# Unrolled rounds of 512 samples, eight looked-up tables, and gathers paced by TensorE's progress in a DLRM tower on one core

## What is computed

```python
e = jnp.stack([tbl_0[ids[:, 0]], ..., tbl_25[ids[:, 25]]], axis=1)
combined = jnp.concatenate([dense[:, None, :], e], axis=1)          # 2048 x 27 x 128
inter = jnp.einsum('bfd,bgd->bfg', combined, combined)[:, triu_i, triu_j]
h = jnp.concatenate([dense, inter, dense], axis=1)                  # 128 + 351 + 128
h = jnp.maximum(h @ W_top1 + b_top1, 0.0)                           # 512
h = jnp.maximum(h @ W_top2 + b_top2, 0.0)                           # 256
y = h @ W_top3                                                      # 1
```

## Time and profile before

| | |
|---|---|
| timed runs, us | 488.62, 491.50, 497.02 (median 491.5) |
| span of the profiled execution, us | 791.1 (granted TensorE clock 0.756 of full) |
| PE busy | 487.2 us, 62% |
| PEld busy | 424.6 us, 54% |
| DVE busy | 226.9 us, 29% |
| ACT busy | 262.0 us, 33% |
| POOL busy | 305.1 us, 39% |

### The profile page before, as it was taken

How to read it: one execution, slowest core, us unless ns; L and a number is a source line. 1 busy time by engine, 2 the same in 40 slices (tenths; PEclk the granted TensorE clock), 3 DMA queues, 4 the chain that set the end, 5 groups by cost and what they waited for, 6 DMA issues and landing times.

```text
span 791.1 us, 8476 instructions
## 1 busy us (share of the span) xinstructions
PE 487.2 (62%) x3016; PEld 424.6 (54%) x3016; DVE 226.9 (29%) x296; ACT 262.0 (33%) x632; POOL 305.1 (39%) x327
## 2 busy tenths in 40 slices
PE   6407566526748086580956719476393855939977
PEld 4306556426637085470855518464282745827866
DVE  3207251222313142321413213133131332313231
ACT  1115131512416033160522615025150432405762
POOL 6751707370442606336072541705327071350000
PEclk8757767666959679596886959768596866958997
DMA  5620202110110101111010110101101020010000
GB/s 128 198 72 11 54 7 55 28 52 9 34 37 19 53 1 45 27 24 46 0 50 20 35 35 9 52 10 40 30 17 50 3 53 17 27 43 1 1 1 0
DMA packets 20003, 27.57 MB, mean 35 GB/s; under 512 B 10940, under 2 KB 13508, under 8 KB 19985
## 3 DMA queue, kind: packets, MB, share of 16 engines
q0 software_dynamic: 10240, 20.99, 10.3%
q1 hardware_dynamic: 9728, 6.32, 2.9%
q10 hardware_dynamic: 16, 0.01, 0.0%
HBM read 27.29 MB, written 0.01 MB: 35 GB/s over the span
## 4 chain that ended last, share of the span: by engine, by line
PE 42%; another core or an unknown queue 22%; issue 20%; ACT 12%; DVE 3%; DMA 0%; ACTq 0%; SPq 0%; DVEq 0%
PE gram L415 16%; PE ring L453 12%; PE ring L372 11%; ACT xt L585 6%; ACT pairs_or_h L606 4%; DVE onehot L705 2%; PE idb L361 1%; PE ring L442 1%; PE ring L476 1%; ACT xt L574 1%; ACT A L592 1%; DMA pairs_t_or_h<-in_ids 0%; DVE A L786 0%; DVE x_or_h_split L772 0%
## 5 line engine op out<-in xcount | busy, mean ns | idle before, releaser
L321 POOL DMA_INDIRECT rows<-in_tbl,ids_tile x320 | 304.3, 951 | 401.6 <-PE ring L400 306.7
L415 PE MATMUL gram<-xt 128*128 128x104 f32 x1024 | 161.4, 318 | 31.6 <-issue 28.3
L415 PEld LDWEIGHTS gram<-xt 128*128 128x128 f32 x1024 | 153.1, 233 | 38.5 <-issue 33.6
L372 PE MATMUL ring<-onehot,table_hi 125*128 125x256 f32 x368 | 113.1, 334 | 37.6 <-DVE onehot L705 31.3
L705 DVE TENSOR_TENSOR onehot<-idb,vrow 125x2048 fp32r<-125x2048 f32 x48 | 110.0, 2292 | 59.8 <-remote 47.2
L453 PE MATMUL ring<-x_or_h_split,w_hi 128*128 128x256 f32 (+1 forms) x384 | 95.6, 322 | 47.9 <-issue 40.2
L785 DVE COPY A<-gram 32x208 f32<-32x208 f32 x64 | 32.2, 503 | 309.6 <-remote 171.3
L591 ACT COPY A<-gram 32x208 f32<-32x208 f32 x64 | 32.4, 506 | 244.4 <-remote 163.9
L453 PEld LDWEIGHTS ring<-x_or_h_split,w_hi 128*128 128x128 f32 (+1 forms) x384 | 74.1, 219 | 64.0 <-issue 56.8
L372 PEld LDWEIGHTS ring<-onehot,table_hi 125*128 125x128 f32 x368 | 79.9, 217 | 48.0 <-issue 40.2
L372 PE MATMUL ring<-onehot,table_lo 125*128 125x256 f32 x368 | 103.7, 308 | 1.4 <-issue 1.4
(11 more groups left out here) (46 smaller groups left out, 272.9 us busy)
## 6 DMA issues: line engine op xcount, KB each, us to landing
rows<-in_tbl,ids_tile POOLq DMA_INDIRECT x320
xt<-in_tbl SPq DMA_DIRECT2D x6, 500.0 KB
rows<-in_r_dense_features SPq DMA_DIRECT2D x16, 64.0 KB
A<-in_W_top SPq DMA_DIRECT2D x2, 256.0 KB
xt<-in_W_top SPq DMA_DIRECT2D x2, 256.0 KB
pairs_or_h<-in_W_top SPq DMA_DIRECT2D x1, 512.0 KB
ids_tile<-in_ids SPq DMA_DIRECT2D x16, 13.0 KB
pairs_t_or_h<-in_ids SPq DMA_DIRECT2D x1, 208.0 KB
```

Of the source, the lines that this page charges most:

```text
L321: pool.indirect_dma_start(rows[:, t % 2, 1 + r, :], None, aps[f"tbl_{f}"], bass.IndirectOffsetOnAxis(ap=ids_tile[:, t, f:f + 1].bitcast(U3 ...
L372: last = pe.matmul(ps[:, 0:HALF], part[:, m, k, :], onehot[:, buf, k, :], start=(k == 0 and part is table_hi), stop=(k == KT - 1 and part ...
L415: last = pe.matmul(gram[:, s % 2, g // PER_BANK, col:col + QUAD * NA], four, cols, start=True, stop=True)
```

## The change

The stage list is one straight list without hardware loops, over four rounds of 512 samples, with pieces of several stages laid between each other. Two more tables (15 and 19) are looked up, so 18 are gathered: 288 gathers. A lookup serves 512 samples: 16 matmuls of 512 columns, 32 lookups in all instead of 48. The ids reach PSUM otherwise: SP loads them from a transposed copy of `ids`, broadcast to 128 partitions, and ACT copies them to PSUM, to `idb` and a bank of `gram` in turn. The one-hots are made in four quarters (125x1024) in three slots. The gathered rows live in a ring of 45 rows, with a semaphore for every six gathers of a tile, and each six gathers also wait until PE has filled as many ring banks as `PACE` says. Layers 1 and 2 are plain float32 without a split (`w1`, `w2`, `x`, `h1` whole); `W_top1` has its pair rows permuted on the host, since the looked-up tables now stand last among the features, so ACT stores each bank of transposed rows in one copy. DVE copies three of four product blocks and some strips of the pairs, ACT the rest. Each ring bank has a semaphore of its own. The raw tables are loaded in two pieces, 112 and 13 partitions. The cleared pads of XT are one instruction on DVE.

```diff
-LOOKUP_TABLES = [2, 5, 10, 12, 13, 14]
+LOOKUP_TABLES = [2, 5, 10, 12, 13, 14, 15, 19]
+ROWS = 45
+GROUP = 6
+PACE = [(0, -2.0), (48, 58.0), (138, 166.0), (282, 354.0)]
...
+        def a_round(r):
+            q, last = r - 1, r == NB - 1
+            for m in range(NL):
+                yield "lookup", r, m, 0
+                if q > 0 and m in (0, 1):
+                    yield from layer("layer2", q, 0, m)
+                if q > 0 and m == 2:
+                    yield from layer("layer3", q, 0, 0)
+                if m in (2, 3):
+                    yield from layer("unblock", q, 1, 2 * m - 4, 2 * m - 3)
+                if m == 4:
+                    yield from layer("pairs", q, 1, 0, 1, 2)
+                if m in (5, 6):
+                    yield from layer("layer1", q, 1, m - 5)
+                    yield from rows(r, 0, m - 5)
...
+            for s in range(TSTEPS):
+                yield "products", r, 2, s
+                yield from rows(r, 3, s)
+                yield from layer("unblock", r, 0, s)
...
+    EARLY_CHUNKS = [(2, 1), (3, 1), (3, 3)]
+    def on_vector(r, h, b):
+        return b % 2 == 1 and (h == 0 or r == NB - 1)
...
+                for part in (slice(0, VP16), slice(VP16, VP)):
+                    sp.dma_start(raw[m][part], src[part]).then_inc(raw_landed[m], 16)
...
+            for m in range(3, NL + 1):
+                spread_ids(m)
             W1, W2 = aps["W_top1"], aps["W_top2"]
+            sp.wait_ge(lo_ready, NL)
+            sp.dma_start(w1[:, 0], W1[0:D, :]).then_inc(w1_landed, 16)
...
+            sp.wait_ge(w1_ready, 1)
+            sp.dma_start(w2[:], W2.rearrange("(k p) n -> p k n", p=P)).then_inc(weights_landed, 16)
...
+                    i = k * NG + g
+                    if i >= ROWS and (g == 0 or group_of(i - ROWS) != group_of(i - ROWS - 1)):
+                        pool.wait_ge(ring_filled, filled("rows", *group_of(i - ROWS)))
+                    if i % GROUP == 0 and progress_for(i, k) > 0:
+                        pool.wait_ge(ring_filled, progress_for(i, k))
...
+            def progress_for(i, k):
+                if k == 0:
+                    return 0
+                return min(filled_by(work_before(i)), USE["rows", (k - 1) // T, (k - 1) % T, 0])
...
-                pe.matmul(idb[:, 0:HALF], ident_r[0:NTAB, f:f + 1].to_broadcast([NTAB, P]),
-                          ids_t[:, col], start=True, stop=True).then_inc(idb_ready, 1)
...
+                for c in range(CH):
+                    pe.wait_ge(onehot_ready, CH * u + c + 1)
+                    for k in range(KC):
+                        for part in (table_hi, table_lo):
+                            last = pe.matmul(ps, part[:, m, c * KC + k, :], onehot[:, (CH * u + c) % SLOTS, k, :],
...
-                terms = [(k, rows, wp, xp) for k, rows in blocks for wp, xp in ((0, 0), (1, 0), (0, 1))]
...
+                pe.matmul(ps, w1[:, 0, n * P:(n + 1) * P], x_dense[:, h, :], start=True, stop=False)
...
+                act.copy(idb_bank(m), ids_spread[:]).then_inc(idb_ready, 1)
...
-            with dve.Fori(0, NROUND) as r:
-                play(r, WHOLE, ring_start(r))
```

More of the change, by code:

```diff
@@ new lines, in build @@
+    RING_STAGES = ("rows", "lookup", "unblock", "pairs", "layer1", "layer2", "layer3")
+    WORK = {"rows": 0.44, "lookup": 3.75, "unblock": 0.36, "pairs": 0.22, "layer1": 1.75, "layer2": 1.85, "layer3": 1.0,
+            "products": 1.8}
+    FIRST_LOOKUP = 5.8
+    USE = {}
+    DONE = []
+    done = 6.0
+    for stage in stages():
+        done += FIRST_LOOKUP if stage[0] == "lookup" and stage[1] == 0 else WORK[stage[0]]
+        if stage[0] in RING_STAGES:
+            USE[stage] = len(USE)
+            DONE.append(done)
@@ L399, in transpose_rows @@
                 for i, row in enumerate(XGROUPS[g]):
-                    last = pe.transpose(ps[:, i * P:(i + 1) * P], rows[:, q, row, :], ident[:])
-                last.then_inc(filled_rows, 1)
-            def products(r, h, s):
-                n = STEPS * (2 * r + 1 + h) + s
-                if not isinstance(n, int) or n >= 2:
+                    src = rows[:, (k * NG + row - 1) % ROWS, :] if row else dense[:, k % 2, :]
+                    last = pe.transpose(ps[:, i * P:(i + 1) * P], src, ident[:])
@@ L408, in products @@
+                last.then_inc(ring_filled, 1)
+            def products(r, t, s):
+                n = step_index(r, t, s)
+                if s == 0:
+                    wait_emptied("rows", r, t, NX - 1)
+                if n >= 2:
                     pe.wait_ge(gram_act, n - 1)
@@ L465, in layer2 @@
-            def layer2(H, start, n):
-                ready = [(h1_lo, H1 // P * (H - 1) + k + 1) for k in range(H1 // P)]
-                w = [part[:, :, n * P:(n + 1) * P] for part in w2]
-                split_products(claim(start)[:, 0:HALF], [(k, P) for k in range(H1 // P)], w, h1_split,
-                               ready if n == 0 else None)
-            def layer3(start, after):
-                pe.wait_ge(emptied, after)
-                ps = claim(start)
+                last.then_inc(ring_filled, 1)
@@ new lines, in _ @@
+            for stage, r, a, n in stages():
+                if stage == "lookup":
+                    lookup(r, a)
+                elif stage == "rows":
+                    transpose_rows(r, a, n)
+                elif stage == "products":
+                    products(r, a, n)
+                elif stage == "unblock":
+                    unblock(r, a, n)
+                elif stage == "pairs":
+                    transpose_pairs(r, a, n)
+                elif stage == "layer1":
+                    layer1(r, a, n)
+                elif stage == "layer2":
+                    layer2(r, a, n)
+                elif stage == "layer3":
+                    layer3(r, a)
@@ L816 @@
+N_WEIGHTS = 7
 _OUTS = [((2048, 1), 'float32')]
```

905 lines of the change are left out of this document (397 added, 508 removed).

## The result

The changed kernel takes 455.2 us (median of 4 runs, 453.99 to 457.87) beside 492.35 us of the kernel before (4 runs): ratio 0.927, 95% interval 0.922 to 0.932. Times are medians of all runs of a kernel and ratios are of its undisturbed runs alone, so the two can differ by a per cent. The gain is 37 us; I had forecast 66.5 (425.0 against 491.5). The 455.2 lie above the forecast's own range of 405 to 440, and at the very end of the wide one, 404 to 456. The direction held, the size did not, and one statement under the forecast was plainly wrong.

The account below looks back on a forecast made before the run. PE was taken to set the time, with POOL close behind. PE's 390 us, 12 for gathers and 7 at the end gave 409; 16 kept of the 47 unexplained made 425 us, own range 405 to 440, wide range 404 to 456.

Parts of the forecast that it names:

- In the profiled execution only: Stretches of some 18 us per tile, engines stopped beside twenty gathers, were taken to be absent from timed runs.
- PE sets the time: Whole kernel before: with the lost stretches cut out, PE is close to always busy, with POOL close behind.
- The 47 us unexplained: Kernel before: 491.5 less the sum of 444, put to register work, hand-overs, lower clock; a third, 16 us, kept.
- the lower clock: Rival: half clock in the lookups, where PE waits for each quarter; slower than before, over 501 us, 4 in 100.
- Lookups at 0.216: Matmuls of 512 columns start 0.216 us apart, so 3.46 per lookup: 111 us against 120.
- Layers 1 and 2 at 1.73: A block of layer 1 or 2 in plain float32 takes 1.73 us against 1.44; +14 us over 48.
- Round 0's lookups bound by DVE, 55: PE starts at about 10; DVE's one-hots set seven lookups at 5.9 us and the last takes 3.5: 55 us.
- The rest of round 0 at bare price, 47.4: Round 0 behind its lookups: products 27.2, three tiles of rows 6.3, A 1.6, pairs 0.9, layers 11.4 us.
- One PE wait of 12 us at gather 144: Last rows of the second round: gathered at 187 us, PE there at 175, so PE waits about 12 once.
- Rows behind products, and the transposes of A spread between steps: ACT's copies hide behind product steps: rows 2.1 us a tile against 3.5 (-22), A 1.6 against 4.3 (-21).
- starved lookups: Rival: waits for one-hot quarters add 12 us per round in three rounds, 36 us; 460 us, 14 in 100.
- POOL's pace: Rival: a gather takes 1.40 us in timed runs, gathers end at 407, about 40 follow; 450 us, 1 in 10.

Follow-up runs that it names:

- e1: The kernel before, unchanged, once more under the profiler, on a chip with stalls: profiled 787.2 us, timed 783 to 795 us.
- e5: The changed kernel as it is, on a chip without stalls: 455.7 us against 488.4 of the kernel before, ratio 0.933.
- e16: The changed kernel as it is, on a chip with stalls: 634.1 us against 794.3 of the kernel before, ratio 0.799.
- e15: The kernel before with 2 of the 20 gathers of each tile, on a chip with stalls: 488.2 us against 794.3 of the kernel before, ratio 0.614.
- e17: The changed kernel without any gather, unblocks and pairs of rounds 1 to 3 next to each other at six places, not between products or lookups: 494.3 us.
- e7: The changed kernel with the gathers of the first three tiles only (54 of 288), without stalls: 457.2 us against 455.7 of the changed kernel.
- e18: The changed kernel without any gather, ids of tables 1 to 3 asked for earlier, fourth quarter before lower part, round 0 ordered like later rounds: 428.4 us.

## Why the prediction was right or wrong

- **"In the profiled execution only": wrong.** The stalls are in every run on some chips and in none on others (e1, e5, e16), and come with the gathers (e15). Cutting them out was still the right sum, by luck, since the timed runs were on a chip without. But the test that I put down (a span of about 695) gave 452.2, and my rule would have misled anyone on the other kind of chip, where the change brings 20%.
- **PE sets the time: right.** 90% busy after, and the chain goes 75% through it.
- **The 47 us unexplained: a third kept was about right by accident, the cause was not.** Some 33 of them are half clock, nearly all of it at the uncovered transposes of A (e15; e17 shows the same at six places, 21 us of clock and 20 of waits); the other 14 stay open. I had half clock last in a list of three. 17 us of it stay, where I kept 16, but all of them in round 0. As a rival I had placed the lower clock in the lookups; it was at A's transposes, and it told in favour of the change.
- **Lookups at 0.216: mis-sized.** Measured 0.23, nearer to the trace's own surcharge (0.226) than to the nearest float32 row. 24 lookups of 16 by 0.014 are 5 us. The rule of the Trainium skill that I quoted gives 0.216 and is 6% low here. With its waits for quarters a lookup of rounds 2 and 3 takes 3.9 from its first matmul to the next stage's, not 3.46. The 24 lookups of rounds 1 to 3 take 95.7 us by this measure, where I had 83.
- **A step of products at 1.70: a little short.** It takes 1.77 to 1.96 in rounds 1 to 3, 5 us more over 48 steps.
- **Layers 1 and 2 at 1.73: right** (a block of layer 1 starts at 368.06, the rows behind it at 369.79).

```profile
368.06 0.60 PE L492 MATMUL ring<-x_dense,w 128*128 128x256 f32 x2
368.50 1.46 PE L494 MATMUL ring<-x,w 128*128 128x256 f32 x6
369.79 0.60 PE L441 MATMUL ring<-ident,rows 128*128 128x128 f32 x4
```

- **Round 0's lookups bound by DVE, 55: the step that failed, 16 us.** I took DVE's 5.9 us a table as the pace, the ids as there, and PE's start at 10. PE starts at 12.8 (3 us); the first two lookups take 8.0 and 11.9 because the ids queue behind the tables (8 us); the next five follow the loop of ACT, DVE and PE and take 34.6, some row transposes between them (5 us). As a bound DVE was right: with both causes out, the lookups come 5.7 apart (e18).
- **The rest of round 0 at bare price, 47.4: the second step that failed, 18 us.** I gave the interleaving of the later rounds to round 0, where three and four banks stand together and the unblocks have no cover. The granted clock of 0.90 over 65.8 us is 7 of it, and PE's waits are 10, 7 of them for ACT's copies.
- **One PE wait of 12 us at gather 144: did not come.** PE came to those rows at 216 us and not at 175. Gathers cost nothing on such a chip (e7). The pitch of 1.25 held (0.94 plus 0.30, in all of e16's burst; in the profile after a few single gathers start 1.3 to 1.7 apart).
- **Rows behind products, and the transposes of A spread between steps: right** for rounds 1 to 3. These and the tail came 7.6 us below what I had allowed, but 27 above their bare sum of 287.6: the 35 us that I had added for gathers, hand-overs and the unexplained made up for dearer lookups and products (17), and for waits and a tail that I have not split further.
- **The rivals.** None of them is what happened. POOL did not set the pace (e7), and the one long wait of PE for one-hots after round 0 is 1.62 us, at 140.94, where starved lookups had 36 us. That 455.2 lies next to their 450 and 460, and inside the range up to 456, is luck: that end of the range stood for POOL's pace and for all 47 us kept, not for round 0.
- **Two sums of the prediction do not close.** The other work beside DVE's 35 us is 27.7 + 12 = 39.7, not 39.5, and 409 + 80 does not follow from an unexplained part that grows from 47 to 100. The forecast rests on neither.

## What to carry over

Price the clock as its own term: find the stretches in which the matrix engine waits in small pieces, look at the granted clock of the next 10 us, and value interleaving by both; here the clock was about half of what the uncovered places cost (21 of 41 us in e17). A loop's steady order does not hold for its first pass: write the first pass out and ask for every bank and every load what stands ahead of it in its queue. When a profile's span is more than half again as long as the timed runs, run the same kernel again before deciding that the profiler is the reason.

## What the runs showed of the hardware

The same program, unchanged, takes 488 us on some chips and 786 to 794 on others. On the latter all engines but the one that issues gathers stop, or crawl, from about 9 to 12 us into a burst of 20 gathers until about 5 us after the start of the last one; PE's gaps beside bursts of 6 to 12 were 2 to 8 us or none, beside one of 18 17.7, and with 2 gathers a tile nothing is left of it (488). A 256 KB broadcast load whose median is 3.3 us took 6.9, 11.3 and 17.6 us behind tables issued before it on the same queue. Matmuls of 512 columns in fp32r start 0.23 us apart at the full clock. Where PE's work came in small pieces with waits between them, the granted clock fell to half for 6.8 to 10.2 us though PE was by then busy (all six places of e17); with the same pieces laid between other matmuls it stayed full.
